# First norm of groups 4 to 7 from a turned copy of x, its factors sent through DRAM, and the opening stretch reordered

## The reference

```python
def _tc_rmsnorm(x, t, gw, gb, bw, bb):
    g = (t @ gw.T + gb)[:, None, :]
    b = (t @ bw.T + bb)[:, None, :]
    inv_rms = jax.lax.rsqrt(jnp.mean(x * x, axis=-1, keepdims=True) + EPS)
    return g * x * inv_rms + b
...
x = x + _attention(_tc_rmsnorm(x, t, g1w, g1b, b1w, b1b), Wq, Wk, Wv, Wo)   # 16 heads of 8
return x + _swiglu(_tc_rmsnorm(x, t, g2w, g2b, b2w, b2b), gate_w, hid_w, out_w)
```

## Time and profile before

| | us |
|---|---|
| three timed runs | 257.65, 257.89, 258.99 |
| their median | 257.89 |
| the profiled execution, as timed | 257.42 |
| its span in the trace | 255.6 |
| outside the span | 1.8 |

### The profile page before, as it was taken

The page is one execution under the profiler, slowest core; times in us unless marked ns, Lnnn a source line. Parts: engine busy times, 40 slices in busy tenths (PEclk is TensorE's granted clock), DMA queues, the critical chain, the costliest instruction groups (busy, mean ns, idle before and its releaser), DMA issues.

```text
span 255.6 us, 8235 instructions
## 1 busy us (share of the span) xinstructions
PE 221.2 (87%) x3048; PEld 177.9 (70%) x3048; DVE 202.9 (79%) x490; ACT 163.3 (64%) x352; POOL 111.9 (44%) x183
## 2 busy tenths in 40 slices
PE   2436777879989999899989999999999999899894
PEld 2314545547667868786878877887888778687894
DVE  4646966897899889889988998899888997565673
ACT  5354658676876686669766777567757655666430
POOL 8323852597265254625381516252623232323320
PEclk9995579999999999999999999999999999999998
DMA  5866601530261026100540045004500000000001
GB/s 162 345 169 147 185 4 28 152 85 3 64 166 27 26 64 164 47 23 19 140 124 0 27 112 152 10 27 114 156 6 26 4 26 3 23 3 24 22 21 44
DMA packets 18819, 18.79 MB, mean 74 GB/s; under 512 B 3644, under 2 KB 17980, under 8 KB 18652
## 3 DMA queue, kind: packets, MB, share of 16 engines
q1 hardware_dynamic: 18252, 17.80, 24.7%
q10 hardware_dynamic: 528, 0.46, 0.8%
HBM read 3.22 MB, written 2.10 MB: 21 GB/s over the span
## 4 chain that ended last, share of the span: by engine, by line
PE 45%; issue 24%; POOL 16%; DVE 9%; ACT 4%; ACTq 1%; POOLq 0%; DVEq 0%
PE proj L489 7%; PE pv L427 6%; PE ffn L320 5%; PE ffn L322 3%; PE ffn L321 3%; PE score L410 3%; DVE nmax L756 3%; POOL inv L923 3%; PE raw L383 3%; POOL qp L915 2%; PE tok L442 2%; POOL xn_lo L936 2%; POOL kp L915 2%; POOL xs L929 2%; PE proj L349 2%
## 5 line engine op out<-in xcount | busy, mean ns | idle before, releaser
L756 DVE TENSOR_REDUCE nmax<-raw 128x8 f32<-128x1024 f32 x61 | 74.2, 1216 | 3.0 <-PE raw L383 2.9
L597 ACT ACTIVATE p_s<-score 128x1024 f32<-128x1024 f32 x64 | 65.5, 1023 | 16.1 <-PE score L410 14.9
L427 PE MATMUL pv<-p_s,va 128*32 128x128 f32 x1024 | 41.7, 280 | 1.8 <-ACT xn L615 1.1
L320 PE MATMUL ffn<-xn_hi,ffn_hi 128*128 128x256 f32 x106 | 34.8, 328 | 1.2 <-POOL xn_lo L936 1.2
L626 ACT ACTIVATE th<-ffn 128x256 f32<-128x256 f32 x53 | 20.3, 384 | 19.6 <-PE ffn L322 19.6
L489 PE MATMUL proj<-ffn_out_s,hT 128*128 128x128 f32 x240 | 31.6, 275 | 0.0
L813 DVE SCALAR_TENSOR_TENSOR gated<-th,ffn 128x256 f32<-128x256 f32 x53 | 22.0, 415 | 12.1 <-ACT th L626 11.7
L427 PEld LDWEIGHTS pv<-p_s,va 128*32 128x32 f32 x1024 | 24.7, 109 | 9.2 <-issue 4.0
L936 POOL TENSOR_TENSOR xn_lo<-xn,xn_hi 128x128 fp32r<-128x128 f32 x32 | 14.7, 460 | 34.6 <-DVE xn_hi L804 34.6
L322 PE MATMUL ffn<-xn_hi,ffn_lo 128*128 128x256 f32 x106 | 29.7, 280 | 0.0
L321 PE MATMUL ffn<-xn_lo,ffn_hi 128*128 128x256 f32 x106 | 29.6, 279 | 0.0
(11 more groups left out here) (130 smaller groups left out, 456.0 us busy)
## 6 DMA issues: line engine op xcount, KB each, us to landing
ks<-kp SPq DMA_DIRECT2D x48, 128.0 KB, 2.4
qs<-qp SPq DMA_DIRECT2D x45, 128.0 KB, 2.5
out_y<-x_s SPq DMA_DIRECT2D x16, 128.0 KB, 1.8
x_s<-in_x SPq DMA_DIRECT2D x1, 1536.0 KB, 10.9
qs<-shift SPq DMA_DIRECT2D x64, 4.0 KB
x_s<-in_x SPq DMA_DIRECT2D x2, 256.0 KB, 3.6
ffn_in_s<-in_ffn_in_w SPq DMA_DIRECT2D x1, 512.0 KB, 6.7
qs<-qp ACTq DMA_DIRECT2D x3, 128.0 KB, 3.7
```

Of the source, the lines that this page charges most:

```text
L320: pe.matmul(dst, w_hi, v_hi, start=True, stop=False)
L427: mm = pe.matmul(pv[VW * j:VW * j + VW, (t % 2) * L:(t % 2 + 1) * L], va[vbuf(g)][:, t // 2, at:at + VW], p_s[:, (BEATS * g + t) % PBUF, p ...
L597: act.activation(p_s[:, n % PBUF, :], score[:], ACT.Exp, scale=SCALE).then_inc(s_exp, 1)
L756: dve.tensor_reduce(heads[:, :, t % 2, :], raw_dst(g, t)[:].rearrange("l (e j m) -> l e j m", e=HALVES, j=HQ), AX.X, ALU.max, negate=True) ...
```

## The change

- **The norm of groups 4 to 7 (`TURNED = 4`).** The host passes a second copy of x, `x_t`, with features first. One DMA of 1 MB brings the half that belongs to groups 4 to 7 into `xT_s`. The four steps are now: `a_mean`, `a_inv` as before; `inv_to_row` (SP, offset -27) writes the 128 x 4 factors to a DRAM tensor; `inv_to_all` (SP, -26) waits for that and reads them back into all 128 partitions (256 KB); `a_scale_turned` (POOL, -24 instead of -26) multiplies the turned copy; `a_norm` on ACT reads the product from SBUF. The sixteen PE transposes of these groups, and the waits of `c_score` for them, are gone. The load of `xT_s` stands on SP behind the first `shift_rows`.
- **Values.** `VALUE` goes from -7 to -2, from place 1 to place 6; `a_key` waits for the bank accordingly.
- **`c_tr2` while T - 1 < 10** moves to the next beat, behind `c_score`.
- **The opening.** The first key is made in two halves; on POOL the low part of the weights comes ahead of the second `a_inv`; ACT does the norms of sequences 2 and 3 of group 1 ahead of its three DMA issues; DVE and POOL split the feed-forward weights here and not at T = 4 and 5; `q_rest` of group 1 stands behind two reductions; raw score 5 goes to `raw` and not to `score`; raw scores 6 and 7 move into T = 0 and 1, and the values of group 0 stand in T = 0, ahead of raw score 6.
- **Unread products.** 24 products of a zeroed tile stand at the head of PE's list. Nothing reads them.

```diff
-    MEAN, INV1, SCALE1, XT1, HI1 = -30, -28, -26, -23, -15
-    VALUE, KEY, QUERY = -7, -14, -13
+    MEAN, INV1, SCALE1, XT1, HI1 = -30, -28, -24, -23, -15
+    INVROW, INVALL = INV1 + 1, INV1 + 2
+    TURNED = 4
+    VALUE, KEY, QUERY = -2, -14, -13
...
-            return score if g == 0 and t % 2 and t < BEATS - 1 else raw
+            return score if g == 0 and t % 2 and t < HQ else raw
...
+        def raws_in(T):
+
+            if T < 2:
+                return [(0, BEATS - 2 + T)]
+            return due(T, RAW, BEATS)
...
+            def inv_to_row(g):
+
+                sp.wait_ge(s_inv1, g + 1)
+                if g > TURNED:
+                    sp.wait_ge(s_invall, 16 * (g - TURNED))
+                sp.dma_start(inv_row, inv1[:]).then_inc(s_invrow, 16)
+
+            def inv_to_all(g):
+
+                sp.wait_ge(s_invrow, 16 * (g - TURNED + 1))
+                if g > TURNED:
+                    sp.wait_ge(s_xs1, g)
+                sp.dma_start(inv_all[:], inv_row.rearrange("l b -> (l b)").partition_broadcast(128)).then_inc(s_invall, 16)
...
             shift_rows(0, 0)
+            sp.dma_start(xT_s[:], x_t.rearrange("d b l -> d (b l)")[:, TURNED * W:]).then_inc(s_xturned, 16)
...
+            pe.wait_ge(s_unread, 1)
+            for j in range(HQ):
+                for e, dst in enumerate((score[:, 0:512], score[:, 512:1024], raw[:, 0:512], raw[:, 512:1024])):
+                    pe.matmul(dst[:, j * L:(j + 1) * L], unread[32 * e:32 * e + 31, 0, :],
+                              unread[32 * e:32 * e + 31, 1, :], start=True, stop=True)
...
             for T in range(LAST + 1):
                 for g, t in due(T, 0, BEATS):
                     c_score(g, t)
-                for g, t in due(T, RAW, BEATS):
+                for g, i in due(T - 1, TR2, NB, 2):
+                    if T - 1 < FFN:
+                        c_tr2(g, i)
+                if T == 0:
+                    a_values(0)
+                for g, t in raws_in(T):
                     b_raw(g, t)
...
             a_norm(1, 1)
             a_middle(0, s_qrest, q_rest, qp, s_qmid)
-            stack_high_queries()
             a_norm(1, 2)
             a_norm(1, 3)
+            stack_high_queries()
...
+            def a_scale_turned(g):
+                if g == TURNED:
+                    pool.wait_ge(s_xturned, 16)
+                pool.wait_ge(s_invall, 16 * (g - TURNED + 1))
+                if g < TURNED + 2:
+                    pool.wait_ge(s_xt1, NB * (g - 1))
+                else:
+                    pool.wait_ge(s_xn1, NB * (g - 1))
+                pool.tensor_tensor(xs1[:, g % 2],
+                                   xT_s[:, (g - TURNED) * W:(g - TURNED + 1) * W].rearrange("d (b l) -> d b l", b=NB),
+                                   inv_all[:].rearrange("d (l b) -> d b l", b=NB), ALU.mult).then_inc(s_xs1, 1)
```

More of the change, by code:

```diff
@@ L108, in bass_cond_transformer_block @@
         xs1 = sb("xs1", [L, 2, NB, D])
+        xT_s = sb("xT_s", [D, (G - TURNED) * W])
+        inv_row = nc.dram_tensor("inv_row", [L, NB], F32).ap()
+        inv_all = sb("inv_all", [D, L * NB])
+        unread = sb("unread", [128, 2, 128], F32R)
         xn1 = sb("xn1", [D, 3, NB, L])
@@ L311, in _ @@
                     shift_rows(g, half)
+                for g, _ in due(T, INVROW, since=TURNED):
+                    inv_to_row(g)
+                for g, _ in due(T, INVALL, since=TURNED):
+                    inv_to_all(g)
                 for g, _ in due(T, STACK, since=2):
@@ L354, in a_key, with first_key @@
                 pe.wait_ge(s_lo1, 2 * (g + 1))
-                if g == 0:
-                    pe.wait_ge(s_wlo, 1)
-                elif g > 1:
-                    pe.wait_ge(s_va, g)
+                if g > 1:
+                    pe.wait_ge(s_va, g - 1)
+                if g > 3:
+                    pe.wait_ge(s_fin, WIN * (g - 4) + 1)
                 split_product(key_dst(g)[:], qk_hi[:, 1, :], qk_lo[:, 1, :], xn1_hi[:], xn1_lo[:]).then_inc(s_k, 1)
+            def first_key():
+                pe.wait_ge(s_wlo, 1)
+                for n in range(2):
+                    half = slice(2 * n * L, 2 * (n + 1) * L)
+                    pe.wait_ge(s_lo1, n + 1)
+                    mm = split_product(key_dst(0)[:, half], qk_hi[:, 1, :], qk_lo[:, 1, :], xn1_hi[:, half],
+                                       xn1_lo[:, half])
+                mm.then_inc(s_k, 1)
             def a_query(g):
@@ L492, in d_out @@
                 mm.then_inc(s_y, 1)
+            pe.wait_ge(s_unread, 1)
[3 more added lines that the diff above has]
+                              unread[32 * e:32 * e + 31, 1, :], start=True, stop=True)
+            for j in range(HQ):
+                for e, dst in enumerate((score[:, 0:512], score[:, 512:1024])):
+                    pe.matmul(dst[:, j * L:(j + 1) * L], unread[32 * e:32 * e + 31, 0, :],
+                              unread[32 * e:32 * e + 31, 1, :], start=True, stop=True)
             pe.wait_ge(s_modw, 32)
@@ L543, in _ @@
                 for g, i in due(T, TR2, NB, 2):
-                    c_tr2(g, i)
+                    if T >= FFN:
+                        c_tr2(g, i)
                 for g, _ in due(T, VALUE, since=1):
@@ L668, in _ @@
             a_middle(1, s_krest, k_rest, kp, s_kmid)
+            a_mean(2)
+            zero_fill(va[1][:].rearrange("l b v -> l (b v)"), s_va0[1])
             a_middle(1, s_qrest, q_rest, qp, s_qmid)
[L670 removed]
             a_mean(3)
[L672 to L677 removed]
+            for b in range(NB):
+                a_norm(2, b)
             for T in range(LAST + 1):
@@ L851, in _ @@
             a_hi(1, 1)
+            dve.wait_ge(s_ffnin, 16)
+            dve.tensor_copy(ffn_hi[:], ffn_in_s[:]).then_inc(s_whi, 1)
             zero_values(0)
             a_rest(1, key_dst(1), kp, k_rest, s_khi, s_klo, s_krest)
+            b_max(0, 0)
+            b_max(0, 1)
             a_rest(1, query_dst(1), qp, q_rest, s_qhi, s_qlo, s_qrest)
-            for t in range(HQ):
-                b_max(0, t)
+            b_max(0, 2)
+            b_max(0, 3)
             b_shift(0, 0)
-            for t in range(HQ, BEATS - 1):
-                b_max(0, t)
+            b_max(0, 4)
+            b_max(0, 5)
             for T in range(LAST + 1):
@@ L1034 @@
         "x": x.transpose(1, 0, 2),
+        "x_t": x.transpose(2, 0, 1),
         "cond": cond.T,
```

78 lines of the change are left out of this document (41 added, 37 removed).

## The result

The changed kernel takes 260.6 us (median of four executions, 259.77 to 261.71) against 257.8 before: a ratio of 1.0096, 95% interval 1.006 to 1.0131. It is slower by 1%, 2.5 to 2.8 us, where 257.0 was forecast. The profiled execution took 260.57 us with a span of 258.8, so that 1.8 us lie outside the span, as before.

A forecast was written before the change was run, and what follows sets the result against it. DVE's chain was taken to bound places 1 to 3, PE places 0, 4, 5 and 6. Opening -1.0 plus steady +0.35 gave -0.65 us, so median 257.89 becomes 257.2, put at 257.0; range 253.4 to 259.6.

The forecast's parts named there:

- Steady beats: From T = 10 on: fewer transposes against values moved to place 6, in sum +0.35 us.
- Rival A: PE bounds every place, so all transposes count and values cost the same anywhere: 252.4 us, chance 0.2.
- rival B: Place 7: `c_tro` still waits, so the values' new beat is paid in full: 260.4 us, chance 0.12.
- The opening: Start up to T = 11: rows carried forward, -1.0 us, between -1.8 and +1.5 by the trip's length.
- up to the score of T = 0: Opening: earlier first and second key bring the score of T = 0 1.3 us earlier than 32.83.
- the maxima give most of it back: Opening: new order of maxima, raw scores and group 0 values leaves group 2's key only 0.8 us early.
- from the key to T = 4: Opening: with group 2's key 0.8 us early, T = 4 starts 0.35 us early.
- c_tr2 no longer holds the next score: T = 4 to 10: score not held while ACT copies; T = 10 would start 1.7 us early.
- the trip of group 4: T = 10 to 11: factors through DRAM take 4.2 us, bounds 3.6 and 7; T = 11 starts 1.0 us early.
- C: Rival: group 4's trip through DRAM takes 7 us and delays POOL's steps at T = 9: 260.0 us, chance 0.1.
- Rival D: Opening: unread products raise the clock, first to second key at twice the pace: 255.5 us, chance 0.13.
- a second key later than 18.5 us: Opening: sign that the carried sum would be off; the second key was forecast near 17.7 us instead of 20.02.

The follow-up runs named there:

- c_maxima: Changed order of raw scores, maxima and group 0 values, added to the kernel before with other opening edits and turned norm for groups 5 to 7; ratio 0.9997.
- a_values0: Changed kernel with the values of group 0 behind raw score 6 at T = 0, not ahead of it; 260.31 us, ratio 1.0075 to the kernel before.
- b_tr2: Kernel before with only the move of `c_tr2` behind the next score until the first FFN piece; 257.87 us, ratio 1.0008.
- a_turned5: Changed kernel with group 4's first norm as before, only groups 5 to 7 through the turned copy and DRAM; 258.8 us, ratio 1.0025 to the kernel before.
- a_nounread: Changed kernel without its 24 unread products and their fill; 260.05 us, ratio 1.0076 to the kernel before.
- b_fill: Kernel before with 140 unread products put into PE's gaps in the opening; 257.44 us, ratio 0.9975.

## Why the prediction was wrong

**Steady beats: right.** T = 32 to 39 +0.16 as forecast, T = 40 to 47 +0.43 (+0.4), T = 48 to 55 -0.19 (-0.1); T = 11 to 31 -0.23 in all (-0.1), but there +0.31 up to T = 16 and -0.54 behind it cancel, which is luck. The mechanism is the one that was read from the earlier trace rows. PE in the changed kernel at T = 33, the key at T = 34, and T = 36; then the values in place 6, T = 39 and T = 40:

```profile
142.07 0.40 PE L453 MATMUL score<-qs,ks 64*128 64x128 bf16 x8
...
144.50 0.40 PE L453 MATMUL score<-qs,ks 64*128 64x128 bf16 x8
...
147.65 0.50 PE L354 MATMUL proj<-xn_hi,qk_hi 128*128 128x512 f32 x1 [0.39 <-POOL xn_lo L988]
...
152.17 0.40 PE L453 MATMUL score<-qs,ks 64*128 64x128 bf16 x8
...
158.75 0.40 PE L453 MATMUL score<-qs,ks 64*128 64x128 bf16 x8
...
161.01 1.06 PE L381 MATMUL proj<-attn_w_s,xn 128*128 128x128 f32 x8
162.00 0.40 PE L453 MATMUL score<-qs,ks 64*128 64x128 bf16 x8
163.13 0.33 PE L485 MATMUL tok<-ident,o_s 128*128 128x128 f32 x1
165.21 0.40 PE L453 MATMUL score<-qs,ks 64*128 64x128 bf16 x8
```

Place 1 is down from 3.44 to 2.43 us, the key now waits 0.39 us for POOL's low part, and places 1 to 3 take 10.10 us together as before. Place 6 has 3.25 us, place 7 3.21 and no wait ahead of `c_tro`. Rival A (PE bound everywhere) wanted less than 9.6 us for places 1 to 3 and falls; rival B (a wait before `c_tro`) falls too. The page that the prediction names for rival A does not back it: the Trainium skill, Perfetto Trace Analysis (Identifying the Most-Contended Engine), excepts TensorE from the rule of the highest occupancy and judges it by its useful work (MFU) and by the busy share of its weight loads. In the window T = 32 to 39 the weight loads (PEld) are busy for 21.25 us and DVE for 23.75.

**The opening: wrong, and by a sum carried.** -1.0 at T = 11 was forecast, +3.28 came. By the prediction's own terms:

| stretch | forecast | measured |
|---|---|---|
| up to the score of T = 0 | -1.3 | -1.64 |
| from there to the key of group 2 ("the maxima give most of it back") | +0.5 | +1.82 |
| from the key to T = 4 | +0.45 | +1.76 |
| T = 4 to 10 ("c_tr2 no longer holds the next score") | -1.35 | +0.11 |
| T = 10 to 11 (the trip of group 4) | +0.7 | +1.23 |
| sum | -1.0 | +3.28 |

Three terms in the middle failed, each by 1.3 to 1.5 us; in the first the step was named and mis-sized, the second left the clock out, the third had its mechanism wrong.

- Up to the first score the sum held: the second key was forecast at 17.7 and came at 18.32, the first raw score at 21.9 and came at 22.03.
- The maxima. The order of raw scores, maxima and values of group 0 was taken as 0.5 us. It measured 1.82 in the changed kernel, and c_maxima prices it at 1.03%, 2.7 us. DVE's wait of 2.48 us spans the values of T = 0, 2.07 us at 1.2 GHz between the score that DVE doesn't need and the raw score that it does. But moving the values alone behind it (a_values0) brought nothing that can be told, so that which part of the new order costs is not shown.
- From the key to T = 4. The sum has no term for the clock here. Key and beat 3 run at 1.2 GHz in the changed kernel: the key product and its two followers take 1.58 us where the kernel before takes 0.87, beat 3 takes 4.52 where it takes 3.47. In b_values, which has only the values moved, T = 2 starts 0.69 us early, but the half pace goes on to 45.9 us (39.3 before), and T = 4 starts 1.22 us late.
- T = 4 to 10. b_tr2 is level with the kernel before, so moving `c_tr2` wins nothing. At T = 6 and T = 8 the turn of the second norm (`d_xt2`) waits 0.60 to 0.68 us for POOL's scale or ACT's copy, whatever the place of `c_tr2`.
- The trip: mechanism right, size wrong. 5.98 us for 4.2, inside the bounds of 3.6 and 7; the scale at 1.53 us for a bound of 1.03 to 2.03. The start of the trip was forecast at 54.2 us and was 56.47, since it hangs on the opening. The prediction's own sum would make its range -1.6 to +1.8 for trips of 3.6 and 7 us, where it has -1.8 to +1.5.

In number two rivals came nearest, B with 260.4 and C with 260.0. For B that is luck, since its wait is not there. C had the trip at 7 us, and a_turned5 prices the trip's part at 0.7%, less than a third of the three prices together. (B and C have chances of 0.12 and 0.1, already more than the 0.2 that the prediction gives to slower.)

The rule on small transfers that was weighed there (the Trainium skill, DMA: Bandwidth & Descriptors, Specifications) would have gone to the upper bound. The trace does not bear that out. The DMA view of 50 to 66 us has, with KB and us from issue to landing:

```profile
inv_all<-inv_row SPq DMA_DIRECT2D x1, 256.0 KB, 3.9
inv_row<-inv SPq DMA_DIRECT2D x1, 2.0 KB, 1.6
```

The write with its pieces of 16 bytes took 1.6 us where 1.8 was taken (the four writes have a median of 2.3, the 16 stores of `out_y` one of 2.2). What was mis-sized is the spread over 128 partitions, 3.9 us for 2.4.

**The unread products.** Rival D (the clock goes up) falls: the first key took the pace of 1.2 GHz, and a_nounread can't be told from the changed kernel. Far more of them do raise the clock (b_fill), and that brought 0.25%.

The named sign, "a second key later than 18.5 us, by which the hand-carried opening would be off", did not warn: the second key was in time, and the error came behind it.

## What to carry to other kernels

A beat's slack read from the profile held to 0.1 us for the windows from T = 32 on; where the orders of five engines change at once, the sum was off by 4 us, though each start it was built from was read right. In such an opening ask of each step that is moved ahead of another who waits for the one behind, and test the new order as a whole: DVE stood idle for 2.48 us where values that nobody needed yet stood ahead of its raw score, but only taking back the whole order, not the values' place alone, brought the 1%. Ask too at which clock the moved work will run; the rows of the kernel before do not say. And a transfer with a fixed trip is a floor under its beat: it takes back what is gained ahead of it, so that it should be left out for the first group that has no slack (a_turned5), while the later groups can have it.
